# Two normalisations' last pass moved to ScalarE, and four exponentials put before any inverse, in the pooled stage of a two-layer kernel

## The reference

```python
h = (x - mu) * rsqrt(var + 1e-5) * ln_g + ln_b          # first norm
query, keys, values = lin(h, Wq, bq), lin(h, Wk, bk), lin(h, Wv, bv)
qw = exp(lin(query, Wqa, bqa) * scale)
qw = qw / cumsum(qw, axis=1)
pooled_query = cumsum(qw * query, axis=1)
mixed_keys = pooled_query * keys
kw = exp(lin(mixed_keys, Wka, bka) * scale)
kw = kw / cumsum(kw, axis=1)
pooled_keys = cumsum(kw * mixed_keys, axis=1)
x = layernorm(x + pooled_keys * values)                 # second norm
x = layernorm(x + dense(x))                             # silu(x Wg) * (x Wu), then Wd
x = layernorm(x + attention_like(x)); x = layernorm(x + experts(x))
```

## Time and profile before

| | us |
|---|---|
| runs (3): median, lowest, highest | 3091.38, 3089.47, 3094.47 |
| the profiled execution | 3089.98 |
| its span on the core | 3088.2 |
| mean granted clock of TensorE | 0.991 of full speed |

### The profile page before, as it was taken

How to read it: one execution, slowest core, us unless ns; L and a number is a source line. 1 busy time by engine, 2 the same in 40 slices (tenths; PEclk the granted TensorE clock), 3 DMA queues, 4 the chain that set the end, 5 groups by cost and what they waited for, 6 DMA issues and landing times.

```text
span 3088.2 us, 38042 instructions
## 1 busy us (share of the span) xinstructions
PE 3007.3 (97%) x13984; PEld 2460.8 (80%) x13984; DVE 1864.4 (60%) x2642; ACT 1174.0 (38%) x2548; POOL 1114.9 (36%) x742
## 2 busy tenths in 40 slices
PE   8998999999999999999999999799999999999997
PEld 7776888888788888888888888678888888888885
DVE  5988433333689999999999999742222222222225
ACT  5544212212366666666666666222111112211110
POOL 6776322222244444444444444212222222322221
PEclk9999999999999999999999999899999999999999
DMA  3001100000222222222222222210100000000001
GB/s 128 1 21 44 40 22 21 21 21 8 73 75 59 69 59 69 59 72 73 69 59 69 59 69 62 65 62 21 41 21 21 21 21 21 27 35 21 1 1 55
DMA packets 61850, 135.39 MB, mean 44 GB/s; under 512 B 9184, under 2 KB 9568, under 8 KB 60512
## 3 DMA queue, kind: packets, MB, share of 16 engines
q1 hardware_dynamic: 61664, 132.95, 14.2%
HBM read 90.71 MB, written 8.65 MB: 32 GB/s over the span
## 4 chain that ended last, share of the span: by engine, by line
PE 89%; DVE 8%; issue 1%; ACT 1%; POOL 0%; DMA 0%; SPq 0%; POOLq 0%; DVEq 0%; ACTq 0%
PE A L44 7%; PE A L45 7%; PE B L44 7%; PE A L46 7%; PE B L45 7%; PE B L46 7%; PE S L44 6%; PE S L45 6%; PE S L46 6%; PE OP L44 5%; PE OP L46 5%; PE OP L45 5%; PE T L1083 2%; PE S L1067 2%; PE O L1077 2%; PE T L44 2%
## 5 line engine op out<-in xcount | busy, mean ns | idle before, releaser
L581 POOL TENSOR_TENSOR ffn_in_lo<-ffn_inner,ffn_in_hi 128x512 fp32r<-128x512 f32 x192 | 250.6, 1306 | 1126.5 <-ACT ffn_in_hi L577 1126.5
L577 ACT ACTIVATE ffn_in_hi<-ffn_inner 128x512 fp32r<-128x512 f32 x192 | 121.3, 633 | 572.3 <-DVE ffn_inner L593 373.2
L44 PE MATMUL S<-xT_hi,ffn_w_hi 128*128 128x512 f32 x768 | 304.0, 396 | 0.0
L46 PE MATMUL S<-xT_hi,ffn_w_lo 128*128 128x512 f32 x768 | 303.7, 395 | 0.0
L45 PE MATMUL S<-xT_lo,ffn_w_hi 128*128 128x512 f32 x768 | 303.7, 395 | 0.0
L593 DVE TENSOR_TENSOR ffn_inner<-B,ffn_gated 128x512 f32<-128x512 f32 x64 | 44.3, 692 | 301.0 <-PE B L46 293.5
L593 DVE TENSOR_TENSOR ffn_inner<-S,ffn_gated 128x512 f32<-128x512 f32 x64 | 44.3, 692 | 299.8 <-PE S L46 299.4
L1625 POOL TENSOR_TENSOR lag_rnorm<-lag_norm,minus_half 128x8 f32<-128x8 f32 x64 | 105.4, 1647 | 304.2 <-DVE lag_norm L1883 304.2
L44 PE MATMUL B<-xT_hi,lag_w_hi 128*128 128x512 f32 x512 | 209.0, 408 | 0.0
L44 PE MATMUL A<-xT_hi,lag_w_hi 128*128 128x512 f32 x512 | 207.9, 406 | 0.0
L46 PE MATMUL B<-xT_hi,lag_w_lo 128*128 128x512 f32 x512 | 203.0, 396 | 0.0
(11 more groups left out here) (390 smaller groups left out, 8055.4 us busy)
## 6 DMA issues: line engine op xcount, KB each, us to landing
lag_raw<-in_head_weights SPq DMA_DIRECT2D x64, 256.0 KB, 4.6
lag_b_row<-lag_b_scratch SPq DMA_DIRECT2D x64, 256.0 KB, 3.4
lag_rot_q<-lag_r SPq DMA_DIRECT2D x128, 128.0 KB, 2.4
lag_rot_k<-lag_r SPq DMA_DIRECT2D x128, 128.0 KB, 2.4
ffn_raw<-in_expert_gate SPq DMA_DIRECT2D x16, 512.0 KB, 3.6
ffn_raw<-in_expert_up SPq DMA_DIRECT2D x16, 512.0 KB, 4.5
ffn_raw<-in_expert_down SPq DMA_DIRECT2D x16, 512.0 KB, 5.3
ffn_raw<-in_dense_gate SPq DMA_DIRECT2D x8, 512.0 KB, 3.6
```

Source lines behind the costliest of these rows:

```text
L44: pe.matmul(out, lh, rh, start=first and k == 0, stop=False)
L46: done = pe.matmul(out, ll, rh, start=False, stop=last and k == n - 1)
L577: act.activation(self.in_hi[t % 2][:, f, :], self.inner[f], ACT.Copy).then_inc(self.s_hhi, 1)
L581: pool.tensor_tensor(self.in_lo[t % 2][:, f, :], self.inner[f], f32(self.in_hi[t % 2][:, f, :]), ALU.subtract).then_inc(self.s_hlo, 1)
```

## The change

It has four parts. First, the last pass of both norms, x * rstd + (-mean * rstd), goes to ScalarE as an Identity activation with scale and bias per row (`ScalarNorm.normalise`). Only batch 0's first norm stays on VectorE (`first_rows`). GpSimd's `root` has a second instruction, the product for the bias. Second, the statistics of the first norm of all four batches, and their roots, are in the prologue. Third, in the first softmax (`qa`), ScalarE does four exponentials before the eight inverse steps, and VectorE four running sums before any reciprocal. Fourth, the transposes of batch 2 use OP0, OP1, A and B, and the first down projection OP0, OP1, T and O, whose row tiles 2 and 3 wait for the second step of reciprocals 2 and 3. The tables of 4 numbers per batch get a place in memory of their own. The core of the diff:

```diff
-        order = [(self.SUM, 0), (self.SUM, 1), (self.FIRST, 0), (self.FIRST, 1), (self.SECOND, 0), (self.SECOND, 1),
-                 (self.SUM, 2), (self.SUM, 3), (self.GAINED, 0), (self.GAINED, 1), (self.TOTAL, 0), (self.TOTAL, 1),
...
+        inverted = both(self.FIRST, (0, 1)) + both(self.SECOND, (0, 1))
+        self.order = {kind: {step: n for n, step in enumerate(both(self.SUM, (0, 1)) + middle + sum(rest, []))}
+                      for kind, middle in (("qa", sums + inverted), ("ka", inverted + sums))}
...
+    def features(self, b, k):
+
+        return b * (TPB + KC) + TPB + k
...
+    def first_normalise(self, act, b):
+        until(act, self.s_hlo, b * KC)
+        self.first.normalise(act, b, self.xn, self.s_hf)
...
+    def first_rows(self, dve):
+        dve.wait_ge(self.first.s_std, 2)
         for t in range(TPB):
+            dve.tensor_scalar(self.xn[:, t, :], self.row(0, t), self.first.rstd[:, t:t + 1], self.first.bias[:, t:t + 1],
+                              ALU.mult, ALU.add).then_inc(self.s_hf, 1)
...
+class ScalarNorm(Norm):
...
+    def root(self, pool, g):
+        pool.wait_ge(self.s_stat, self.of(g, 2 * TPB + 2))
+        pool.tensor_tensor(self.cols(self.rstd, g), self.cols(self.std, g), self.mem["minus_half"][:, 0:TPB],
+                           ALU.pow).then_inc(self.s_std, 1)
+        pool.wait_ge(self.s_std, 2 * g + 1)
+        pool.tensor_tensor(self.cols(self.bias, g), self.cols(self.mean, g), self.cols(self.rstd, g),
+                           ALU.mult).then_inc(self.s_std, 1)
+
+    def normalise(self, act, g, out=None, done=None):
+        act.wait_ge(self.s_std, 2 * g + 2)
+        for t in range(TPB):
+            j = g * TPB + t
+            act.activation(self.row(g, t) if out is None else out[:, t, :], self.row(g, t), ACT.Identity,
+                           bias=self.bias[:, j:j + 1], scale=self.rstd[:, j:j + 1]).then_inc(done or self.s_row, 1)
...
-        ENDS = [OP0, OP1, OP0, OP1]
+        LOOSE, FREED = [OP0, OP1, A, B], [OP0, OP1, T, O]
...
-                turn0.turn(pe, 2, ENDS, norm0.s_row, lambda t: pe.wait_ge(turn0.s_lo, 2 * TPB + t - 1), (2, 3))
-                dense.down(pe, 0, 0, lambda tt: pe.wait_ge(*((turn0.s_lo, 2 * TPB + tt + 3) if tt < 2 else
-                                                             (dense.s_acc, tt - 1))), ENDS)
+                turn0.turn(pe, 2, LOOSE, norm0.s_row, lambda t: pe.wait_ge(dense.s_h, FPU + 1), (2, 3))
+                dense.down(pe, 0, 0, lambda tt: pe.wait_ge(*((turn0.s_lo, 2 * TPB + tt + 1) if tt < 2 else (
+                    pooled.s_step["ka"], pooled.step("ka", BATCH - 1, tt, pooled.SECOND) + 1))), FREED)
...
                 for m in range(KC):
                     pooled.query_high(act, 0, m)
+                pooled.first_normalise(act, 1)
                 for m in range(KC):
                     pooled.key(act, 0, m)
...
+                def first_softmax(b):
+                    for m in range(KC):
+                        pooled.exponential(act, "qa", b, m)
+                    for pair in PAIRS:
+                        pooled.inverses(act, "qa", b, pair)
...
                     for m in range(KC):
                         pooled.query(act, b + 1, m)
-                    softmax("ka", b, b + 1)
+                    if b + 2 < BATCH:
+                        pooled.first_normalise(act, b + 2)
+                    softmax(b, b + 1)
                     for m in range(KC):
                         pooled.key(act, b + 1, m)
+                    if b:
+                        norm0.normalise(act, b - 1)
...
                     pooled.query_low(pool, 0, m)
                 pooled.weight_low(pool, 3, pooled.s_wlo_p)
-                pooled.first_root(pool, 1)
+                for b in range(1, BATCH):
+                    norm_x.root(pool, b)
...
-                pooled.first_statistics(dve, 1)
-                pooled.first_normalise(dve, 1)
+                for b in range(1, BATCH):
+                    pooled.first_statistics(dve, b)
 
                 for b in range(BATCH - 1):
-                    pooled.sums(dve, "qa", b, (0, 1))
+                    pooled.sums(dve, "qa", b, range(KC))
                     pooled.reciprocals(dve, "qa", b, (0, 1))
-                    pooled.sums(dve, "qa", b, (2, 3))
                     pooled.gained(dve, "qa", b, (0, 1))
```

More of the change, by code:

```diff
@@ L96, with __init__ @@
     SUM, FIRST, SECOND, GAINED, TOTAL = range(5)
-    N1 = 4 * TPB
-    def __init__(self, nc, mem, places, banks, norm):
+    def __init__(self, nc, mem, places, banks, norms):
         sem = Sems(nc, "pool")
-        self.mem, self.norm = mem, norm
+        self.mem, (self.first, self.norm) = mem, norms
         self.x_tok, self.ident, self.half = mem["x_tok"], mem["ident"], mem["minus_half"][:, 0:TPB]
@@ L141, in place, with step @@
         return self.at[kind, b] + m
-    def step(self, b, m, n):
-        return b * len(self.order) + self.order[n, m]
+    def step(self, kind, b, m, n):
+        return b * len(self.order[kind]) + self.order[kind][n, m]
+    def features(self, b, k):
+        return b * (TPB + KC) + TPB + k
     def part(self, kind, b, m):
@@ L178, in turn @@
     def turn(self, pe, b, chunks):
-        pe.wait_ge(self.s_n1, b * self.N1 + self.N1)
+        pe.wait_ge(self.s_hf, self.features(b, 0))
         if b == 0:
@@ L1352, in softmax @@
                                 pooled.query_high(act, split, m)
-                        pooled.inverses(act, kind, b, pair)
+                        pooled.inverses(act, "ka", b, pair)
+                def first_softmax(b):
[3 more added lines that the diff above has]
+                        pooled.inverses(act, "qa", b, pair)
                 for b in range(BATCH - 1):
-                    softmax("qa", b)
+                    first_softmax(b)
                     for k in range(KC - 1):
@@ L1395, in _ @@
                 dense.inner_hi(act, 0, 1, 1)
-                step(dense, 0, 2)
+                dense.silu(act, 0, 2, 0)
+                dense.inner_hi(act, 0, 2, 0)
+                dense.silu(act, 0, 2, 1)
+                norm0.normalise(act, last)
+                dense.inner_hi(act, 0, 2, 1)
                 act.wait_ge(pooled.s_out["ka"], BATCH * KC)
@@ L1534, in mean_root @@
                     pool.tensor_tensor(ms[:, cols], ms[:, cols], half[:, cols], ALU.pow).then_inc(s_root, 1)
-                pooled.first_root(pool, 0)
+                norm_x.root(pool, 0)
                 for k in range(KC):
@@ L1762, in _ @@
                 dense.dequantise(dve, 0)
-                pooled.sums(dve, "qa", last, (0, 1))
+                pooled.sums(dve, "qa", last, range(KC))
                 pooled.reciprocals(dve, "qa", last, (0, 1))
-                pooled.sums(dve, "qa", last, (2, 3))
                 pooled.gained(dve, "qa", last, (0, 1))
@@ L1792, in _ @@
                 pooled.totals(dve, "ka", last, (2, 3))
-                dense.add(dve, 0, 0, ENDS)
+                dense.add(dve, 0, 0, FREED)
                 dense.dequantise(dve, 1)
```

117 lines of the change are left out of this document (56 added, 61 removed).

## The result

The changed kernel takes 3044.77 us (median of 4 runs, 3043.74 to 3047.97) where the kernel before takes 3092.05 (4 runs, 3089.47 to 3094.47): 47 us less, ratio 0.9849, 95% interval 0.9832 to 0.9866. I had written 3088.3, with 3081 as the low end. The profiled execution took 3044.13 (span 3042.4, 1.7 around it).

The account below looks back on a forecast made before the run. TensorE, busy 97% of the span, bounds the kernel; only idle time and low-clock stretches can be won. Terms 0.3 + 7.0 + 1.0 + 0.3 - 1.8 - 1.9 - 8.0 = -3.1 us give 3088.3, range 3081 to 3095.

Parts of the forecast that it names:

- +0.3 of the first root: Prologue, batch 0: GpSimd's added bias product lies on the path to the first transpose, +0.3 us (0 to +1).
- start to V0 (new stop for key 0): Up to batch 0's value products: TensorE waits for key 0 behind batch 1's normalisation, +7.0 us (+5.5 to +8).
- V0 to V1: Value products of batch 0 to batch 1: low part of feature 3 comes late, +1.0 us (0 to +2).
- V1 to V2: Value products of batch 1 to 2: new feature and low-part stops against 3.3 us removed, +0.3 (-2 to +2).
- V2 to V3: Value products of batch 2 to 3: stops of 3.0 us replace 4.8, -1.8 us (-4.8 to 0).
- V3 to M (batch 3, down projection): From batch 3's value products to the first gate product behind the third down projection: batch 3 -1.9, down projection -8.0 us.
- The first softmax: Batches 0 to 2: stops for exponentials go, feature and low-part waits come; +1.0, +0.3 and -1.8 us.
- The replay: Hand-worked VectorE queue: scans of 1.17 us take turns with GpSimd operations of 1.27; adds and multiplies 0.6.
- rival (a): VectorE and GpSimd turns cost less than replayed; more stops vanish, total -13.8 us, 3077.6; chance 0.15.
- Rival (b): Batch 0: stop for key 0 absent or half as long; -6.6 to -10 us, about 3083; chance 0.12.
- (c): Batches 0 to 2: features one more turn late, clock falls; 12 us on top, +8.9, 3100; chance 0.1.
- (d): Down projection's 8 us given back as ScalarE waits for batch 3's root; up to +5, 3096; chance 0.08.

Follow-up runs that it names:

- the kernel with the keys first: Changed kernel with ScalarE's normalisation of batch 1 moved behind the keys of batch 0: 3037.04 us, ratio 0.982.

## Why the prediction was wrong

The step that failed is one term that was not there. My sum ended at the down projection, and every product behind it, and every product at all, kept the duration that it had before; the new place of the tables in memory got no price, without a reason. The section on the change names it ("a place in memory of their own"), but not that it shifts everything above them. It is worth 43.3 us in the kernel before, and 41.9 us of the measured difference lie behind M. By stages, from traces: from M to the last gate product of the dense layer 8.4, from there to the first of the experts 13.9, to the end 19.7. The experts' part is a count: 3,072 products with `xT` x 6.7 ns = 20.6. The 3,072 of the lag layer lose only 4.3 ns each; that they stand in short runs between smaller matmuls may be why, which no run tested. The evidence lay in the earlier trace rows: 0.40 us for the value product at 48.13 and for the gate product at 304.76, 0.39 for the attention product at 37.22, one shape, and lengths that differ. I took 0.227 for some products and 0.23 for others and did not ask why.

The rest of the sum, against the same places of the traces, counted from the first q product (the +0.3 of the first root lies ahead of it and can't be told in these traces). The sum knew nothing of the placement, so the fair column is the last: the changed kernel with the tables 32 bytes up, against the kernel before.

| step | predicted | changed kernel | changed, tables 32 bytes up |
|---|---|---|---|
| start to V0 (new stop for key 0) | +7.0 | +8.4 | +7.7 |
| V0 to V1 | +1.0 | -0.1 | 0.0 |
| V1 to V2 | +0.3 | -1.3 | -1.3 |
| V2 to V3 | -1.8 | -2.5 | -2.6 |
| V3 to M (batch 3, down projection) | -9.9 | -8.2 | -8.8 |
| sum | -3.4 | -3.7 | -5.0 |

- **The new stop** came as worked out. GpSimd and ScalarE of the changed kernel, in order of time: the power at 37.97 after the low part of the v weights, the small product at 0.20 (I had 0.3), the four passes at 2.93 (I had 2.8, and 2.9 by the Trainium skill, ScalarE: Activation LUTs, whose figures stand under What ACT_TABLE_LOAD costs; the trace agrees with it), then the key at 42.19.

```profile
33.42 4.58 POOL L306 TENSOR_TENSOR pool_w_v_lo<-pool_vf,pool_w_v_hi 128x2048 fp32r<-128x2048 f32 x1
37.97 1.00 POOL L508 TENSOR_TENSOR norm_x_rstd<-norm_x_std,minus_half 128x4 f32<-128x4 f32 x1
39.05 0.20 POOL L511 TENSOR_TENSOR norm_x_bias<-norm_x_mean,norm_x_rstd 128x4 f32<-128x4 f32 x1
```

```profile
39.35 2.93 ACT L518 ACTIVATE pool_xn<-x_tok,norm_x_bias,norm_x_rstd 128x512 f32<-128x512 f32 x4 [10.08 <-POOL norm_x_bias L511]
```

  The product followed at 43.00 where I had 42.65. The clock fell as in the earlier trace rows, here to 0.50 for the whole of 43 to 47 us, and cost 2.4 rather than 1.6: from the first attention product to V0 took 13.35, not 10.91.

```profile
43.00:47.00 4.00, 4.00 (x10) 3.13 (x11) 0.00 (x0) 1.57 (x3) 0.00 (x0) 0.50 0.00 0
```

- **The first softmax** was right in kind: stops for `pool_xn` in two parts, 1.32 and 0.61 in batch 1 where I had 2.4. Of the low parts one was late, by 0.8. The replay was too pessimistic in each batch, by 1.1, 1.6 and 0.7 (1.0, 1.6 and 0.8 in the old placement); rival (a) went that way, but much further. That rival misread a row: the two scans at 109.54 took 2.33 while GpSimd stood idle until 110.83, so they don't show that turns cost less. That the reciprocal steps pass GpSimd freely held: two took 1.26 at 242.28 and the next two 1.27, while GpSimd worked from 236.99 to 244.68.
- **Batch 3 and the down projection** gave 8.2, not 9.9 (8.8 in the old placement). The down projection was right: from the transposes ahead of it to the next gate product TensorE took 14.86 before (289.90 to 304.76) and 7.25 after (293.96 to 301.21), 7.6 less where 8.0 was forecast, and in place of 4.46 and a fallen clock 0.61 of waiting is left, where at most 0.65 was forecast. Keeping the old banks cost only 5.9 (5.2 by the medians), because the stop is shorter there, 3.93, and the clock fell less: 0.74 in 302 to 306 us, against 0.50 in 299 to 303 before. Batch 3 was mis-sized: up to those transposes 0.3 was gained and not 1.9 (1.2 in the old placement). The stop at the turned tiles of `xT` (4.31 at 247.78) is the one that I expected to take back what OP gives, and the four sums of VectorE took 6.66 (7.2 expected, with three gains between). But the second attention products at 271.17 wait 1.83 for a low part, where they waited 0.46 before and 0.51 with the tables 32 bytes up. Ahead of that low part VectorE has a small step that the change adds, the negated mean (L504). It took 1.34 at 266.73, until GpSimd was through with the low part of the mixed keys (268.05), and 0.16 in the trace with 0.51. The other seven traces of kernels with this step show 1.33 to 1.35, and a wait of 1.82 to 1.85. So a step of 128x4 that the sum had at nothing goes with 1.3 of TensorE's time.
- **Rival (b)**, no stop for key 0, was wrong in the kernel and is what the kernel with the keys first makes of it: I had priced it 3.5 to 7 below the forecast, and 7.7 were measured. Rivals (c) and (d) did not come. (d), with its 3096, also lay outside the range that was said to take it in.

So without the placement the kernel moved by 3.8 us where 3.1 was forecast (by the traces 5.0 up to M, but that trace is of the fastest of ten runs, and the one without the 1.3 of the small step), and it measures 3088.08 against the 3088.3 of the forecast. That agreement is in part luck: the new stop cost 0.7 to 1.4 more than forecast and the way from V3 to M gained 1.1 to 1.7 less, against 3.4 by which the first softmax came out better, and the interval of the medians, 1.5 to 7.4, is wide. What was forecast was the change without its placement.

## What to carry to other kernels

Where a change adds or removes a tensor in SBUF, compare the start addresses of all operands of the engine that bounds the kernel, before and after, and not only its instructions: 32 bytes were worth eleven times the change's own 3.8 us. Put weights and moving tensors of float32r products with 512 columns at the same place modulo 256 bytes; an odd size of a small table ahead of them is enough to lose it. And where equal instructions differ by some ns in one trace (0.39 and 0.40 here), ask what sorts them before counting waits: here 6.7 ns each outweighed all of the stops, on an engine that is 97% busy.

## What was not expected of the hardware

- A 128x512 product in float32r starts 226.7 to 227.5 ns after the one before where weights and moving tensor lie a multiple of 256 bytes apart, and 232.3 to 234.0 where the weights lie 16 to 160, 224 or 544 bytes above. By the Trainium skill (TensorE: Matmul & The Clock Gate, Back-to-back issue gap) the gap of a single matmul is N / 2.4 plus 2.5, 216 ns at 512 columns, and a stream of weight loads and matmuls has one per 131 ns; no stretch here shows less than 226.7, and the page speaks of no placement.
- It isn't the distance modulo 256 alone. Weights at +192 give 228.8, but the moving tensor at +64, the same distance, 233.3; 8 and 4 bytes give 230.7 and 232.3, 240 gives 228.5, 252 gives 226.8, and both at +16 230.0. The law behind these values stays open, and so does whether it is a matmul's own weights or the next whose place counts: one half of the test says the next, the other half is between.
- Aligned products are not at 226.7 at once. Behind the stretch of 128 columns the first intervals of the last aligned stretch of 512 took 280, 230, 231, 236, 228, 233 and 231 ns, and then 226 or 227, so that the whole stretch comes to 228.2. In the kernel before, each down projection behind its slow gate products begins with five such intervals (230, 236, 228, 233 and 230 at 402.8 us); in the changed kernel they are at 226 or 227 from the first (at 413.5).
- Products of 256 and 128 columns don't pay it, at the one distance that was tried with them, 32.
- A small instruction of VectorE can last as long as a large one of GpSimd beside it: while GpSimd made the low part of the v weights (33.42 to 38.00), a step of 128x4 took 3.05 us, to 38.03, and 0.17 after it (VectorE of the changed kernel, in order of time). The statistics of four whole tiles took 2.46 both beside GpSimd (at 32.21) and after that instruction (at 38.02). That the small steps wait for GpSimd is read from the times and not tested. The 3.05 cost nothing here, the 1.34 of the second norm's step of batch 2 goes with TensorE's wait before 271.17.

```profile
34.98 3.05 DVE L503 TENSOR_SCALAR norm_x_std<-norm_x_mv 128x4 f32<-128x4 f32 x1
...
40.79 0.17 DVE L503 TENSOR_SCALAR norm_x_std<-norm_x_mv 128x4 f32<-128x4 f32 x1
...
266.73 1.34 DVE L504 TENSOR_SCALAR norm_mean<-norm_mv 128x4 f32<-128x4 f32 x1
```
